# A small attention layer with an fp8 product beside it: three shared result banks, the normalisation on VectorE, one end for each batch, and new instruction orders

## The reference

```python
xn  = layernorm(x)                               # over the 256 features, eps 1e-5
kqv = xn @ Wqkv + bqkv                           # 16 heads of 16; q, k, v
scores = einsum('bsnh,btnh->bnst', k, q) / 4
scores = triu(scores) + -10000 * tril(ones, k=-1)
attn = softmax(scores, axis=2)
out  = einsum('bnkq,bknh->bqnh', attn, v) @ Wo + bo
ffn  = fp8_round(xn / input_scale) * input_scale @ (w8 * weight_scale).T
y    = x + out + ffn
```

## Time and profile before

| | |
|---|---|
| runs shown, us | 281.4 and 284.94, median 283.17 |
| the profiled execution, us | 286.0, its span 284.3 |
| busy: PE, PEld, DVE, ACT, POOL | 72%, 54%, 49%, 37%, 55% |
| mean granted TensorE clock | 0.862 of full |
| chain that ended last | PE 51%, DVE 19%, POOL 14%, issue 8%, ACT 6%, DMA 1% |
| moved by DMA | 20.59 MB, mean 72 GB/s |

### The profile page before, as it was taken

One profiled execution on the slowest core, in us unless ns is written; L12 is line 12 of the kernel. 1 busy time (PEld: TensorE's weight loads), 2 busy tenths in 40 slices (PEclk: granted clock), 3 DMA queues, 4 the chain that ended last, 5 costly groups with the idle time before them and its releaser, 6 DMA issues.

```text
span 284.3 us, 4678 instructions
## 1 busy us (share of the span) xinstructions
PE 205.1 (72%) x1668; PEld 154.0 (54%) x1668; DVE 139.2 (49%) x265; ACT 104.1 (37%) x171; POOL 155.1 (55%) x352
## 2 busy tenths in 40 slices
PE   5196633847886597968785779766987869958945
PEld 5175532636755285746463656655765646635613
DVE  3836832567766144747671164529454743421220
ACT  4122300323530444246424434154416524635410
POOL 7472394496482866458737936386627433443320
PEclk9997965865995977999999697999799986986977
DMA  6619939759282006520661025703370010010011
GB/s 162 180 26 202 200 69 158 207 95 122 59 140 36 0 0 113 101 58 1 111 117 40 2 60 96 112 0 68 71 127 2 5 39 0 6 37 0 2 37 37
DMA packets 24444, 20.59 MB, mean 72 GB/s; under 512 B 2589, under 2 KB 24166, under 8 KB 24422
## 3 DMA queue, kind: packets, MB, share of 16 engines
q1 hardware_dynamic: 23024, 19.18, 35.9%
q10 hardware_dynamic: 1398, 1.12, 1.5%
HBM read 3.22 MB, written 2.10 MB: 19 GB/s over the span
## 4 chain that ended last, share of the span: by engine, by line
PE 51%; DVE 19%; POOL 14%; issue 8%; ACT 6%; DMA 1%; DVEq 0%; POOLq 0%; ACTq 0%
PE bankB L917 8%; PE ps L864 6%; PE bankA L978 5%; DVE row_max L661 5%; PE pso L889 5%; POOL xn L258 4%; ACT probs L473 3%; POOL probs L387 3%; PE bankB L924 3%; PE ps L847 2%; PE ps L843 2%; PE ps L849 2%; PE pso L895 2%; PE bankB L907 2%; PE bankA L924 2%
## 5 line engine op out<-in xcount | busy, mean ns | idle before, releaser
L661 DVE TENSOR_REDUCE row_max<-ps 128x4 f32<-128x1024 f32 (+1 forms) x48 | 58.5, 1221 | 64.7 <-PE ps L849 35.9
L387 POOL TENSOR_SCALAR_AFFINE_SELECT probs<-probs 128x256 f32<-128x256 f32 x128 | 49.1, 413 | 49.9 <-ACT probs L473 49.7
L473 ACT ACTIVATE probs<-ps 128x1024 f32<-128x1024 f32 x48 | 49.1, 1023 | 18.3 <-PE ps L864 13.8
L864 PE MATMUL ps<-q_stack,k_stack 99*128 99x256 bf16 x128 | 23.9, 319 | 11.6 <-ACT probs L473 11.6
L405 POOL TENSOR_TENSOR y<-y,x_all 128x256 f32<-128x256 f32 x16 | 11.2, 724 | 33.9 <-ACT y L528 33.9
L917 PE MATMUL bankB<-xT,wqk_sb 128*128 128x256 f32 x64 | 22.4, 511 | 8.0 <-ACT xs L522 7.9
L847 PE MATMUL ps<-k_stack,q_stack 96*128 96x128 bf16 x128 | 21.4, 244 | 6.5 <-DVE row_max L661 6.3
L864 PEld LDWEIGHTS ps<-q_stack,k_stack 99*128 99x128 bf16 x128 | 13.1, 113 | 18.6 <-ACT probs L473 14.6
L917 PEld LDWEIGHTS bankB<-xT,wqk_sb 128*128 128x128 f32 x64 | 16.3, 267 | 11.8 <-issue 7.3
L849 PE MATMUL ps<-k_stack,q_stack 125*128 125x128 bf16 x128 | 21.4, 243 | 0.0
L495 ACT ACTIVATE o_raw<-pso 128x512 f32<-128x512 f32 x16 | 9.6, 597 | 27.9 <-PE pso L895 27.9
(11 more groups left out here) (132 smaller groups left out, 391.8 us busy)
## 6 DMA issues: line engine op xcount, KB each, us to landing
q_stack<-q_parts SPq DMA_DIRECT2D x48, 128.0 KB
k_stack<-k_parts SPq DMA_DIRECT2D x48, 128.0 KB
x_all<-in_L_attn_x_dram SPq DMA_DIRECT2D x8, 256.0 KB, 5.7
out_dram<-y SPq DMA_DIRECT2D x8, 256.0 KB, 2.1
k_stack<-fixed_k SPq DMA_DIRECT2D x4, 256.0 KB, 5.4
q_stack<-fixed_q SPq DMA_DIRECT2D x4, 256.0 KB, 6.0
wqkv_sb<-in_L_attn_Wqkv_dram ACTq DMA_DIRECT2D x3, 256.0 KB, 4.0
wo_sb<-in_L_attn_Wo_dram ACTq DMA_DIRECT2D x1, 256.0 KB, 4.3
```

The source lines that it names most:

```text
L387: ins = pool.affine_select(out=v[:, h:h + 2], in_=v[:, h:h + 2], compare_op=ALU.is_ge, fill=0.0, base=0, pattern=[[0, 2], [1, P]], channel ...
L473: act.activation(probs[:, i, :], ps2[:], ACT.Exp, scale=SCALE).then_inc(exp_done, 1)
L661: dve.tensor_reduce(dst, src, AX_X, ALU.max).then_inc(max_done, 1)
L864: mm = pe.matmul(ps2[:, h * S:h * S + S], k_stack[0:K_SOFT, s, hh, 0:P], q_stack[0:K_SOFT, s, hh, :], start=True, stop=True)
```

## The change

Every shared product gets a fixed bank out of three (BANK). pso shrinks from one bank for each half to one bank for both; PSUM stays full. `normalise` runs on VectorE for every batch. The first three groups of inverse deviations (ROOTS) come from a square root on ScalarE (`root`) and four VectorE instructions, the fourth group from the old 14 steps on GpSimd. xs has three buffers. The two halves' sums go into one tile, and division, transposes back and copy are done once a batch. The bias of the output moves from VectorE's first loop turn to a product ahead of the loop and GpSimd. The orders of all five lists are new. Of the diff, the core:

```diff
+BANK = {"xT": "C", "q": "A", "o1": "B", "k": "C", "suffix": "A", "norm": "B", "max": "C", "v": "A", "o0": "B",
+        "ffn": "C", "proj": "A"}
-        xs = sb("xs", [P, 2, KT, S])
+        xs = sb("xs", [P, 3, KT, S])
-        pso = psum("pso", [P, 2, 2, S])
-        bank = {"A": psum("bankA", [P, 512]), "B": psum("bankB", [P, 512])}
+        pso = psum("pso", [P, 2, S])
+        bank = {name: psum(f"bank{name}", [P, 512]) for name in "ABC"}
...
+            if g < ROOTS:
+                eng.wait_ge(root_ready, g + 1)
+                then(eng.reciprocal(r, std[:, lo:hi]))
+                then(eng.scalar_tensor_tensor(out=a, in0=v, scalar=-0.5, in1=r, op0=ALU.mult, op1=ALU.mult))
+                then(eng.tensor_tensor(a, a, r, ALU.mult))
+                then(eng.scalar_tensor_tensor(out=r, in0=a, scalar=1.5, in1=r, op0=ALU.add, op1=ALU.mult))
+                return
...
             first_parts(1)
             other_parts(1)
+            max_to_stack(0)
+            load_x(5)
+            first_parts(2)
             load_fixed(2)
-            for b in range(4, B):
-                load_x(b)
-            first_parts(2)
-            max_to_stack(0)
             other_parts(2)
+            load_x(6)
+            load_x(7)
             load_fixed(3)
...
             for n in range(LAST):
-                p = n + AHEAD
-                if p < B:
-                    norm(p)
+                p, f = n + AHEAD, n + 1
                 causal(n, 0)
+                causal(n, 1)
+                if p < B:
+                    split(pool, p, "q", 2)
+                causal(n, 2)
                 if p - 1 < B:
                     round_x(p - 1)
...
                 causal(n, 4)
-                if n + 1 < B:
-                    residual(n + 1)
-                if n in (0, 2):
-                    inverse_std(pool, 3 + n // 2)
+                if f < B and n > 0:
+                    residual(f)
                 causal(n, 5)
+                if n == 0:
+                    inverse_std(pool, 3)
+                if n == 0:
+                    residual(0)
+                    residual(1)
...
+            def root(g):
+                lo, hi = TB * XG[g][0], TB * XG[g][1]
+                act.wait_ge(var_ready, g + 1)
+                act.activation(std[:, lo:hi], var_eps[:, lo:hi], ACT.Sqrt).then_inc(root_ready, 1)
...
+            act.activation(warm[:], var_eps[:, 0:1], ACT.Exp, scale=-1.0)
...
                     exponentials(n, 5)
+                if f < B:
+                    ffn_out(f)
...
+            def norm(b):
+                wait(dve, xT_mm, b - 1)
+                g = [lo <= b < hi for lo, hi in XG].index(True)
+                dve.wait_ge(rstd_step[g], 4 if g < ROOTS else 14)
+                normalise(dve, b).then_inc(xn_ready, 1)
...
+                if p < B:
+                    norm(p)
                 if f < B:
                     maxima(f, 3)
...
+                if a >= 0:
+                    sum_o(a, 1)
+                if p < B:
+                    rest1(p, "q")
                 if f < B:
                     maxima(f, 5)
                     negate_and_split(f)
+                if n == 0:
+                    clip(1)
+                if a >= 0:
+                    divide_o(a)
+                if p < B:
+                    rest1(p, "k")
+                if live:
+                    masked_part(n)
...
+                if a >= 0:
+                    add_up(a)
```

More of the change, by code:

```diff
@@ L713, in add_up, with divide_o @@
-            def add_up(b, bk):
+                src = bank[BANK[f"o{half}"]][:].rearrange("p (t h e) -> p t h e", t=TB, h=HALF)[:, :, :, 0:NVC]
+                heads = slice(HALF * half, HALF * half + HALF)
+                dve.tensor_tensor(o_sum[:, :, heads], src, o_masked[:, b % 2, :, heads], ALU.add).then_inc(norm_step, 1)
+            def divide_o(b):
+                dve.wait_ge(norm_step, 4 * b + 2)
+                dve.reciprocal(o_den[:], o_sum[:, :, :, HD]).then_inc(norm_step, 1)
+                dve.wait_ge(norm_step, 4 * b + 3)
+                wait(dve, oT_mm, b)
+                dve.tensor_tensor(o_tok[:].rearrange("p t (h d) -> p t h d", d=HD), o_sum[:, :, :, 0:HD],
+                                  o_den[:].unsqueeze(3).to_broadcast([P, TB, H, HD]), ALU.mult).then_inc(norm_step, 1)
@@ L876, in values @@
                 if j == 0:
-                    wait(pe, o_raw_ready, 2 * (b - 1) + half + 1)
+                    if b == 0 and half == 0:
+                        pe.wait_ge(ob_ready, 1)
+                    wait(pe, o_raw_ready, 2 * b + half)
                     pe.wait_ge(v_ready, b + 1)
-                    if b == 0:
-                        pe.wait_ge(w8T_ready, 1)
                 s = b % STACKS
@@ L984, in _ @@
                 pe.transpose(ps1[:, 0:P], ident[:], ident[:])
[L985 removed]
+            transpose_x(0)
             pe.wait_ge(b_ready, 1)
@@ L989, in _ @@
             pe.wait_ge(wqk_ready, 1)
-            project_qk(0, "q", "B")
-            project_qk(0, "k", "A")
+            project_qk(0, "q")
+            project_qk(0, "k")
             pe.wait_ge(wv_landed, 16)
-            project_v(0, "B")
-            transpose_x(1, "B")
-            project_qk(1, "q", "B")
-            project_qk(1, "k", "A")
-            project_v(1, "B")
+            project_v(0)
+            transpose_x(1)
+            project_qk(1, "q")
+            pe.wait_ge(b_col_ready, 1)
+            project_qk(1, "k")
+            pe.wait_ge(bv_ready, 1)
+            pe.wait_ge(wo_landed, 16)
+            for k in range(KT):
+                mm = pe.matmul(pso[0:PARTS, 0], bv_cols[:, k], wo_sb[:, k], start=(k == 0), stop=(k == KT - 1))
+            mm.then_inc(bias_mm, 1)
+            project_v(1)
+            phase1(0, 0)
+            transpose_x(2)
+            phase1(0, 1)
+            phase1(0, 2)
+            project_qk(2, "q")
+            phase1(0, 3)
+            phase1(0, 4)
+            phase1(0, 5)
+            project_qk(2, "k")
+            transpose_max(0)
+            phase1(1, 0)
+            project_v(2)
+            phase1(1, 1)
             pe.wait_ge(w8_ready, 1)
```

410 lines of the change are left out of this document (186 added, 224 removed).

## The result

| | before | after |
|---|---|---|
| runs, us | 281.4, 284.94 | 224.78, 223.92 |
| median, us | 283.17 | 224.35 |
| ratio, 95% interval | | 0.792 (0.770 to 0.815) |
| profiled execution, its span, us | 286.0, 284.3 | 224.78, 223.1 |
| mean granted clock | 0.862 | 0.921 |

Later, beside experiment 7 and two repeats, four runs of it gave a median of 224.32, ratio 0.792 (0.787 to 0.798). The forecast was 217 in a range of 205 to 240.

What follows compares the result with a forecast made beforehand. No engine was full; TensorE's waits, four of 5.87 us in a batch, were taken to bound the kernel. Prologue 47, five batches 112, light batches 33.5, end 26 make 218.5; + 1.7 - 2.8 gives 217 us, range 205 to 240.

Steps and rivals of the forecast that it cites:

- the conversion: End of the sum: from profiled span to median of runs, 1.7 us added around the span and 2.8 taken off.
- signs named: Trace signs for right (TensorE over 90% busy, batches of 21 to 22 us, loop before 50) or wrong (loop after 55).
- x0 is normalised at 8.4, not 12.0: Prologue: square root and four VectorE steps replace 14 steps, ready at 6.0 to 7.6, so q starts at 10.4.
- early q of batch 2: Prologue: x2 normalised on VectorE at 26.4 and a third xs buffer let this product start at 30 for 47.27.
- this case at 1 in 5: VectorE's normalisation and GpSimd exclude each other: x0 1.8 us later, up to 0.72 a batch, 222 us for 217.
- The transfers' rival: Prologue bound by transfers: stacks and fixed rows queue, maxima's rows land late, loop starts at 56, 226 us; chance 0.11.
- The four waits: TensorE's waits in a batch, for xn 1.12, k_rest 2.09, y 1.06, probs 1.60, together 5.87 us; all would go.
- gone, barely: The k_rest wait: division done at 10.5 us into the batch, TensorE's groups ahead of the output's transposes about 11.0.
- The added wait: GpSimd's residual ahead of the last masks needs ffn_out: 5.1 us against TensorE's 4.9, so 0.2 us of wait.
- slower than before: Rival: residual ahead of the masks makes them a whole turn late, batches of 39 us, 311 in all; chance 0.03.
- for the two that are near: Batches 2 to 4: 0.5 us allowed for two close waits, in 21.5 = 20.84 + 0.2 + 0.5.
- batches at 28: Rival that waits only move, to suffix and the maxima's transposes: 249 us, 268 with the prologue unmoved; chance 0.03.

Runs made afterwards that it cites:

- experiment 7: The changed kernel with GpSimd's last causal masks put ahead of the residual: 222.53 us, the changed kernel beside it 224.32.
- Experiment 1: The changed kernel with GpSimd held at its last two fixed masks, and the fill of v behind them, until x0 is normalised: 217.51 us, again 216.25.
- experiment 2: The changed kernel with its new orders, but the loop's shared products back in the two banks of before: 245.44 us, ratio 0.871.
- experiment 3: The kernel before, with its old orders and GpSimd normalisation, given the three banks and one bank for the values' products: 256.92 us, ratio 0.912.
- version 1: The kernel of Experiment 1: the changed kernel with GpSimd's last two fixed masks waiting for x0's normalisation; 217.51 us, again 216.25.
- experiment 4: The kernel before, with only the normalisation of batches 3 to 7 moved from GpSimd to the head of VectorE's turn: 275.49 us, ratio 0.978.
- experiment 5: The changed kernel, with only the normalisation of batches 3 to 7 moved back to the head of GpSimd's turn: 240.77 us, ratio 0.862.
- version 8: The kernel of experiment 8: version 1 with maxima's rows in bank B and two batches' fixed masks loaded earlier; 216.37 us, again 213.53.
- experiment 8: Version 1 with the maxima's rows in bank B and the fixed masks of batches 2 and 3 loaded ahead of the first maxima's rows: 216.37 us, again 213.53.
- experiment 9: Version 8 with the inverse deviations in five groups and x3, x4 loaded behind the first stack: 224.97 us, ratio 0.803.

## Why the prediction was right, and where it was not

By its sum, forecast against measured: prologue 47 and 55.2, five batches 112 and 108.0, two light ones 33.5 and 33.2, last batch and end 26 and 26.7. Together 218.5 and 223.1: the sum is 4.6 off because the prologue, mis-sized by 8.2, was partly made good by the batches, which is luck. Another 2.4 of the 7 us between 217 and 224.35 come from the conversion: the deduction of 2.8 for the profiled execution, taken over from before, measured 0.4 here. Of the signs named, the batches' were met (TensorE busy 94 to 98% in batches 2 to 4, no wait for k_rest or y, none in the loop for normalised rows), and a loop start before 50 was not. The last one, 24 us or less between the starts of the last two stages, was not met either: they lie 33.2 apart, as the forecast's own 33.5 has it.

*The prologue.* The step that failed is "x0 is normalised at 8.4, not 12.0". The square root and its four steps were ready at 7.2, earlier than I had it; but x0 was ready at 12.5, since the two tiles ran 5.24 us beside GpSimd's masks and fill. Experiment 1 takes away that neighbour alone: x0 is ready at 8.0, batch 2's q starts at 32.2 (forecast 30, measured 37.77), and the loop at 46.72, where the forecast had 47. The total then is 216 to 217.5. That this is the forecast's 217 is in part luck: 4 us less in the batches make up for the deduction of 2.8, which did not apply.

The prediction put the early q of batch 2 down to the normalisation and the third xs buffer. They do it without the third bank (37.35 in experiment 2), but the third bank does nearly as much without them (38.30 in experiment 3; 47.27 before, 37.77 in the changed kernel).

The prediction had this case at 1 in 5 with 1.8 us at x0. The Trainium skill, SBUF — State Buffer, section "SBUF: two separate sides", on which that rested, says that when VectorE's instruction is in a two-port mode, the engine that starts first holds a shared pair of memory ports for its whole instruction and the other waits. The prologue agrees in part (5.24 us against 0.74 with GpSimd idle, the second tile ending 0.16 behind the fill). But the first tile began 0.25 us ahead of the mask of 2.53, behind an earlier one that kept its 0.40, and took 2.53 itself, which the rule does not give. And in the loop such a tile ran from 122.93 to 123.34 in 0.41 us while GpSimd's masks ran until 123.17 and from 123.12, in 0.41 and 0.47 (GpSimd's spans are rough in the profile). Here the measurement decides: as far as these rows go, not every such pair excludes each other. The up to 0.72 us a batch that I had reckoned for the loop did not come.

*The transfers' rival* (loop at 56, 226 us) gave nearly the measured numbers, and a loop start after 55 was what I had named as "wrong". The number alone would have spoken for it, and the DMA share rose to 1.05. Experiment 1 shows where it begins: with the list of transfers as it was, holding GpSimd alone starts the loop 8.5 us sooner. But the rival is not all wrong. TensorE waited 3.39 us for batch 0's stack, which the prediction had argued against, and 1.91 for batch 1's; only the second is gone in version 1.

*The four waits.* xn, y and probs vanish and k_rest's turns into 0.39 for the division: "gone, barely" (forecast: ready at 10.5, wanted at 11.0; measured: 11.5 and 11.2). Experiments 2 to 5 show that none of the parts tried does it alone. An undisturbed batch takes 26.71 before, 24.70 with the banks, 24.74 with the orders and the normalisation, 22.29 with banks and orders, 20.54 with all. So the banks give 2.0 by themselves and 4.2 on top of the rest: with the old orders, two of the waits that go are in part replaced by others for a bank. The normalisation gives about as much either way, 1.3 by itself (experiment 4, ahead of the drop in clock) and 1.8 on top. The orders without the normalisation, the joined ends and the third xs buffer were not taken apart.

*The added wait.* "0.2 us, nothing to spare" was right twice: moving the residual behind the masks gives 0.1, and 3.3 us more in its place cost 3.3 and a lower clock. So lateness on GpSimd's path does reach TensorE, as the rival "slower than before" has it; masks that come a whole turn late were not seen.

*The batches.* Forecast 23.5, 24, 21.5, 21.5, 21.5; measured 24.43, 21.02, 21.47, 20.54, 20.54. In batch 1 I feared a wait of 2.37 for masks behind 14 steps, and a normalisation on VectorE that waits for them. The second was a misreading: batch 1's turn normalises x4, whose inverse deviation comes from the square root (third group of XG), and did so at 80.53; the 14 steps serve x5 to x7. GpSimd does them in batch 1 from 80.77 to 84.70, where TensorE has maximum and value products of its own, and the last masks stand ahead of them: TensorE waits 0.31 for a mask in all of it. In batches 3 and 4 the half microsecond "for the two that are near" was not needed. The forecast took 20.84 us of TensorE's work for each batch, that of an undisturbed one, though the five held 114.42 in all; now they hold 100.30. An undisturbed batch's work fell only from 20.82 to 20.15, so about 10.8 of the 14.1 us (an estimate) are the clock, granted at 0.97 where it was 0.89.

*Side sums.* The high end is 236 by its own terms (217 + 14.5 + half of 9), not 240, and batches at 28 add 28 us, not 32. Neither changes a verdict.

*The table loads.* ScalarE's timeline:

```profile
4.77 1.28 ACT L499 ACT_TABLE_LOAD   x1 [4.77 <-issue]
6.06 0.20 ACT L499 ACTIVATE std<-var_eps 128x2 f32<-128x2 f32 x1
29.06 1.28 ACT L594 ACT_TABLE_LOAD   x1
30.35 0.20 ACT L594 ACTIVATE warm<-var_eps 128x1 f32<-128x1 f32 x1
```

Each costs 1.28 us and the activation behind it starts at once. The Trainium skill, ScalarE: Activation LUTs, section "What ACT_TABLE_LOAD costs", adds a drain of about 1.38 us to every switch. None shows behind either load here, so the 1.4 us by it do not appear.

**Open.** Why batch 1's stack was carried more slowly in the changed kernel than in version 1 is not known. What stretches the first tile and the mask to 2.53 us each is open too. And why the runs of versions 1 and 8 spread more than those of the changed kernel was not settled: they differ in granted clock (0.942 to 0.982 among their profiled executions).

## What to carry to other kernels

Where several waits of a like size stand in one turn, a part of a change may look worth little or nothing alone, because another wait takes its place or because the clock fell; compare batches at the same granted clock, count what TensorE has left when all waits are gone, and try the parts together. Before moving an instruction to VectorE, look at what GpSimd does at that very time: a tile that runs in 0.41 us alone took 2.5 beside a mask and a fill, and holding GpSimd for 1.2 us gave back 8. When a number comes out as a rival's, take away the rival's cause and your own, one at a time, before believing it.

## What the runs showed of the hardware

In the prologue a VectorE normalising tile and a GpSimd mask slowed each other, 0.41 to 2.53 us and 0.40 to 2.53, though neither had to wait for the other's result. Beside GpSimd's fill of v a VectorE instruction of this form (tensor_scalar) ended only behind the fill: the second tile at 12.49 (fill 12.33), the first tile of experiment 7 at 10.51 (10.21), and in version 1 one of 0.19 us that took 1.58 and ended at 11.42 (11.25). Moments that ran beside that same fill kept their 0.74 us. In the loop, beside masks alone, tiles took 0.40 to 0.50 us.

A wait can cost again through the clock. The first q product, after TensorE had waited 5.78 us for x0, took 3.75 in the changed kernel. Where that wait was 1.3 to 1.9 us and the product started at 9.5 to 9.9, it took 1.97, 3.35, 3.48, 2.80 and 3.75 in the profiled executions of experiments 1 (twice), 8 (twice) and 9, the same work at the same place: 1.97 and 3.75 are the two levels (granted clock 1 and 0.5), and what lies between changed level within it. So an earlier start does not by itself bring the higher level.
